# A sparse mixture of experts: routing and row scatter inside the layer norm, fixed regions of rows, a down product that gives rows, and paired value products in attention

## The chip, the cores and the metric

The kernel runs on one core of a Trainium2 chip. The metric is the device time of one launch in microseconds (us), as the median of several runs. Engines are named as the profile names them: PE is TensorE (matmul), PEld its weight loads, DVE is VectorE, ACT is ScalarE, POOL is GpSimd, SP is SyncE, which issues most DMAs.

## The reference

The reference is a small hybrid network on 32 sequences of 256 tokens with 128 channels (8192 tokens), in float32. Its layers, each added to the residual x: a two-way state-space layer, a dense feed-forward with 8 small experts, a recurrence, the feed-forward again, a local attention mixed with a latent one, a sparse mixture of experts, a causal attention, and the sparse mixture again. The change touches the two sparse mixtures and the two attentions. The mixture, cut to what matters:

```python
xn = (xf - mu) * rsqrt(var + 1e-5) * ln_gamma + ln_beta        # 8192 x 128
logits = xn @ router_w                                         # 8 experts
probs = softmax(logits); topv, topi = top_k(probs, 2); topv /= sum(topv)
for e in range(8):                                             # F = 512 hidden
    gate, up = split(xn @ gate_up_w[e])
    out += comb[:, e:e+1] * (silu(clip(gate, -10, 10)) * up @ down_w[e])
out += swiglu(xn, shared_gate_up_w, shared_down_w)             # shared, 128 hidden
```

The attention that the change touches is a softmax over 128 to 256 keys for 16 heads of width 8, per sequence and per 128 queries.

## The kernel before

The residual X and the normed U lie in SBUF for the whole program, channels on the 128 partitions and tokens along the row; 512 tokens are a tile (16 tiles). The program is a series of stages with barriers between them; inside a stage each engine runs a list written out by hand, and semaphores order the engines. Nothing reorders a list: what stands behind a waiting instruction on an engine waits too.

A sparse mixture (`l1_ffn`, twice: called ffn3 after the local attention and ffn4 after the causal one) has three stages and a fourth part:

- `layer_norm` with `route`: per tile, PE forms the mean and the variance (products with a matrix of 1/128, lines 95 and 100) and the logits (line 107), DVE subtracts the mean (129), scales (143) and shifts (146), POOL squares (175), ACT takes logarithm and exponential.
- `route_pairs` with `Choice`: after the last tile, for all 8192 tokens at once, DVE picks the two best experts, counts the tokens of each expert, and computes for each of the 16384 pairs (token, expert) a row number (`plan.slots`) in a table in DRAM, `pairs`, in which every expert's rows start at a multiple of 512. That start depends on the counts of all tokens. It also computes the expert of each of 39 blocks of 512 rows.
- `l1_experts`: chunks 0 to 15 are the shared expert on tiles of U. Meanwhile PE turns the tiles of U to rows (`turn_rows`), ACT copies them into a ring of 4 buffers `sent` (`take_rows`, line 1858), DVE adds 4 numbers for each row (`send_meta`, 1910), and POOL writes rows to `pairs` with indirect DMAs, 128 rows of 528 bytes each, 8 for a tile and 128 in all (line 1750). SP then waits for all of these DMAs and fetches the blocks (`fetch`, 1711). Per block PE turns the rows back (`turn_block`, 1811), and runs 4 chunks: gate and up products (1766 to 1768, three float32r products each), and a down product in plain float32 with the down weights loaded and 512 activations moving (1802). The result has channels on partitions: ACT copies it to `y` (`take_y`, 1876), PE turns it to rows (`turn_y`, 1820), DVE scales the rows (`scale_y`, 1946), and POOL writes them to a second table, `results`, by 4 indirect DMAs per block (1756).
- Last, the two result rows of each token are fetched, added and turned back into X.

Rows of `pairs` that no token takes must lead to spare rows of `results`: two copies of `pairs` are filled ahead of time, during the state-space layer, with zeros and a spare row number, by 6 DMAs (line 328).

In `stacked_attention` each unit of work on PE is a score product (`scores`, 2381, after a mask product 2378), the same turned over (`scores_turned`, 2407), from which ACT makes powers, and a value product (`weigh`, 2421): four heads side by side in the array, 32 columns each, with V loaded and the powers moving. A list `pending` keeps the value products two units behind. There are 384 units per attention.

Of the kernel before, what the change touches and what calls it, by code (L numbers as in the profile page):

```python
# [7 lines left out]
F32 = mybir.dt.float32  # L8
# [6 lines left out]
D = 128  # L15
# [230 lines left out]
def mamba(nc, mem, X, U):  # L246
# [14 lines left out]
    with ExitStack() as ctx:  # L261
# [63 lines left out]
        def _(sp):  # L325
            def fill(i):
                which, r = divmod(i, RING)
                sp.dma_start(mem.scratch["pairs"][which].rearrange("(i r p s) c -> r p i (s c)", r=RING, p=128, s=QUART)[r],
                             mem.empty[:, r, :, :].rearrange("p s c -> p (s c)").unsqueeze(1).to_broadcast([128, NBLK // RING, QUART * ROW])).then_inc(mem.filled, 16)

            for q in range(UNITS):
# [12 lines left out]
                if 4 <= q < 4 + 2 * RING:  # L344
                    fill(q - 4)
# [1090 lines left out]
HELD = 3  # L1436
OUT_ROWS = TOK // D
# [12 lines left out]
def fill_pairs(nc, mem):  # L1450

    empty = mem.empty
    with ExitStack() as inner:
        (zeroed, marked) = inner.enter_context(signals(nc, "fill_rows", "zeroed", "marked"))
        block = inner.enter_context(nc.Block())

        @block.vector
        def _(dve):
            nc.vector.memset(empty[:, :, :, :], 0.0).then_inc(zeroed, 1)
            dve.wait_ge(zeroed, 1 + LEAD)  # L1460
            nc.vector.tensor_copy(empty[:, :, :, ROW - 1], mem.const["spare"].rearrange("p (r s) -> p r s", r=RING)).then_inc(marked, 1)


def pairs_filled(nc, mem):

    with nc.Block() as block:
        @block.sync
        def _(sp):
            sp.wait_ge(mem.filled, 16 * 2 * RING + LEAD)
# [71 lines left out]
def route_pairs(nc, stage, mem, logits, plan):  # L1541

    with ExitStack() as ctx:
        def sb(name, *shape):
            return ctx.enter_context(nc.sbuf_tensor(stage + "_" + name, [128, *shape], F32))
        choice = Choice(nc, ctx, stage, mem, logits)
        chosen, restart, place, picked = sb("chosen", NE, NB), sb("restart", NE, NB), sb("place", NE, NB), sb("picked", NB, NE)
        running = sb("running", NE, NB)  # L1550
        past = sb("past", NE, TOK // BLK)
        needed, ends, base, ones = sb("needed", NE), sb("ends", NE), sb("base", NE), sb("ones", NE)
        slots = sb("slots", 2, NB)
        passed, count, rest = sb("passed", NBLK, NE), sb("count", NBLK), sb("rest39", NBLK)
        (made, counted, prefixed, step) = ctx.enter_context(signals(nc, stage + "_plan", "made", "counted", "prefixed", "step"))
        block = ctx.enter_context(nc.Block())
        by_expert = lambda ap: ap.rearrange("p j e -> p e j")
        by_token = lambda ap: ap.rearrange("p e j -> p j e")
        flat = lambda ap: ap.rearrange("p e j -> p (e j)")

        @block.gpsimd
        def _(pool):
            nc.gpsimd.memset(restart[:, :, :], 1.0).then_inc(made, 1)
            nc.gpsimd.memset(ones[:, :], 1.0).then_inc(made, 1)
            pool.wait_ge(made, 2 + LEAD)
            pool.sem_inc(PASSED[0], 1)
            nc.gpsimd.memset(restart[:, :, 0:1], 0.0).then_inc(made, 1)
            nc.gpsimd.tensor_copy(plan.meta[:, :, 3], mem.w["rows"]).then_inc(made, 1)

        @block.tensor  # L1570
        def _(pe):
            pe.wait_ge(counted, 1 + LEAD)
            nc.tensor.matmul(mem.bank[0][:, 0:NE], mem.w["before"], running[:, :, NB - 1], start=True, stop=True)
            nc.tensor.matmul(mem.bank[0][:, NE:2 * NE], mem.avg, running[:, :, NB - 1], start=True, stop=True).then_inc(prefixed, 1)

        @block.scalar
        def _(act):
            choice.scalar(act)

        @block.vector  # L1580
        def _(dve):
            choice.vector(dve)
            before, share = mem.bank[0][:, 0:NE], mem.bank[0][:, NE:2 * NE]
            nc.vector.tensor_tensor(by_token(chosen[:, :, :]), choice.first[:, :, :], choice.second[:, :, :], ALU.add).then_inc(step, 1)
            dve.wait_ge(made, 4 + LEAD)
            dve.wait_ge(step, 1 + LEAD)
# [1671 lines left out]
```

## Time and profile before

| | us |
|---|---|
| median of 3 runs (5911.37 to 5921.76) | 5917.6 |
| the profiled execution, its own time | 5923.9 |
| its span in the profile | 5922.0 |
| PE busy (share of the span) | 4916.7 (83%) |
| DVE busy | 4141.1 (70%) |
| ACT busy | 3098.6 (52%) |
| POOL busy | 3293.7 (56%) |

The busy shares are means over stages with different limits, so the stretches of the two mixtures and the two attentions are read by themselves. Time outside the span is 1.9 us.

### The profile page before, as it was taken

The numbers are of one execution on the slowest core, as the hardware profiler recorded it, in microseconds if no ns is written. First come the engines' busy times: TensorE is split into PE (matmuls) and PEld (weight loads), VectorE is DVE, ScalarE is ACT, GpSimd is POOL, SyncE is SP. The second block draws the span as 40 slices with busy tenths as digits, with TensorE's granted clock in tenths as the row PEclk, the third lists the DMA queues.
The fourth block names the chain that finished last, engine by engine and source line by source line (L and its number), as shares of the span: only waits on it lengthen the run. The fifth ranks groups of instructions, "written<-read, shape, count | busy, mean of one in ns | idle before, by whom it ended". The sixth has DMA issues, their size and how long they took to land. (4 is left out here: it accounts for less than half of the span.)

```text
span 5922.0 us, 78494 instructions
## 1 busy us (share of the span) xinstructions
PE 4916.7 (83%) x22329; PEld 2499.5 (42%) x22446; DVE 4141.1 (70%) x6054; ACT 3098.6 (52%) x5311; POOL 3293.7 (56%) x2373
## 2 busy tenths in 40 slices
PE   5888888888887788988797999845996899963997
PEld 1333333333333443444353555423663444432664
DVE  5999999999997573058566788633775666642775
ACT  5666666666664464245555777511332577821332
POOL 3888988898895363026343444345334565536333
PEclk8999999999999899999898999967997999976998
DMA  2234322222221002000004333012552444211555
GB/s 81 90 138 151 117 87 90 86 87 90 83 90 47 0 0 87 0 0 0 6 8 96 84 92 90 21 56 83 188 187 96 108 96 102 66 42 51 179 189 172
DMA packets 203031, 494.20 MB, mean 83 GB/s; under 512 B 32432, under 2 KB 57520, under 8 KB 191280
## 3 DMA queue, kind: packets, MB, share of 16 engines
q1 hardware_dynamic: 183536, 451.33, 24.5%
q0 software_dynamic: 18176, 37.79, 1.9%
q8 instruction: 166, 2.72, 0.2%
q14 instruction: 193, 1.58, 0.1%
q10 hardware_dynamic: 960, 0.79, 0.1%
HBM read 381.65 MB, written 108.12 MB: 83 GB/s over the span
## 5 line engine op out<-in xcount | busy, mean ns | idle before, releaser
L396 POOL TENSOR_TENSOR mamba_bu<-mamba_du,mamba_b_all 128x1024 f32<-128x1024 f32 x512 | 1198.6, 2358 | 185.3 <-PE psum L490 170.0
L667 DVE TENSOR_TENSOR_SCAN mamba_bu<-psum,mamba_bu 128x512 f32<-128x512 f32 x1024 | 1190.2, 1207 | 68.3 <-POOL mamba_bu L396 34.0
L490 PE MATMUL psum<-mamba_bu,consts 128*128 128x512 f32 x2048 | 965.4, 594 | 8.3 <-issue 5.1
L599 ACT ACTIVATE psum<-mamba_delta,A 128x510 f32<-128x510 f32 x1024 | 682.9, 683 | 388.8 <-DVE mamba_bu L667 375.7
L1756 POOL DMA_INDIRECT results<-ffn_moe_y_rows,ffn_moe_row_of x312 | 302.0, 968 | 507.2 <-DVE ffn_moe_y_rows L1946 426.3
L1871 ACT ACTIVATE ffn_moe_act<-ffn_moe_act 128x512 f32<-128x512 f32 x344 | 216.9, 631 | 688.8 <-DVE ffn_moe_act L1915 466.2
L673 DVE TENSOR_TENSOR mamba_bu<-mamba_bu,psum 128x1024 f32<-128x1024 f32 x448 | 537.3, 1199 | 5.6 <-remote 1.9
L490 PEld LDWEIGHTS psum<-mamba_bu,consts 128*128 128x128 f32 x2048 | 392.7, 192 | 347.0 <-issue 328.5
L2311 POOL TENSOR_TENSOR loc_q_bd<-loc_q_max,weights_l1a 128x512 fp32r<-128x512 f32 x256 | 274.8, 1102 | 383.4 <-DVE loc_q_max L2566 374.8
L2311 POOL TENSOR_TENSOR cau_q_bd<-cau_q_max,weights_l1b 128x512 fp32r<-128x512 f32 x256 | 258.3, 1042 | 241.4 <-DVE cau_q_max L2566 181.8
L2557 DVE TENSOR_REDUCE cau_top<-psum 128x2 f32<-128x512 f32 (+1 forms) x384 | 263.1, 692 | 181.0 <-PE psum L2381 167.4
L1915 DVE TENSOR_SCALAR ffn_moe_act<-psum 128x512 f32<-128x512 f32 x344 | 237.0, 689 | 206.5 <-PE psum L1768 129.2
L1766 PE MATMUL psum<-ffn_moe_x,ffn_moe_w_gu 128*128 128x512 f32 x624 | 372.1, 596 | 2.9 <-DVE ffn_moe_x L1905 2.9
L1750 POOL DMA_INDIRECT pairs<-ffn_moe_sent,ffn_slots x256 | 252.7, 987 | 158.4 <-ACT ffn_moe_sent L1858 82.2
L2557 DVE TENSOR_REDUCE loc_top<-psum 128x2 f32<-128x512 f32 (+1 forms) x384 | 261.1, 687 | 113.9 <-PE psum L2381 106.0
L1802 PE MATMUL psum<-ffn_moe_act,ffn_moe_w_down 128*128 128x512 f32 x624 | 318.2, 592 | 0.0
L475 PE MATMUL psum<-mamba_parts,consts 128*128 128x512 bf16 x384 | 148.4, 387 | 204.0 <-DVE mamba_bu L673 204.0
L2474 ACT ACTIVATE psum<-consts 128x512 f32<-128x512 bf16 x508 | 305.7, 602 | 16.1
L2378 PE MATMUL psum<-consts 128*128 128x256 bf16 (+1 forms) x1024 | 272.0, 306 | 41.8 <-DVE loc_top L2557 16.8
L2471 ACT ACTIVATE loc_powers<-psum 128x512 f32<-128x512 f32 x384 | 226.6, 591 | 115.2 <-PE psum L2407 114.5
L1920 DVE TENSOR_TENSOR ffn_moe_act<-ffn_moe_act,psum 128x512 f32<-128x512 f32 x344 | 235.6, 685 | 53.4 <-DMA gate_up_parts<-split_parts 30.4
L2471 ACT ACTIVATE cau_powers<-psum 128x512 f32<-128x512 f32 x384 | 225.3, 592 | 80.0 <-PE psum L2407 77.5
(426 smaller groups left out, 11023.6 us busy)
## 6 DMA issues: line engine op xcount, KB each, us to landing
mamba_b_all<-b_rows SPq DMA_DIRECT2D x256, 512.0 KB
ffn_moe_w_gu<-gate_up_parts SPq DMA_DIRECT2D x78, 1024.0 KB
pairs<-empty_rows SPq DMA_DIRECT2D x6, 3432.0 KB, 13.2
ffn_moe_got<-pairs SPq DMA_DIRECT2D x78, 264.0 KB, 3.2
ffn_moe_w_down<-in_l_moe SPq DMA_DIRECT2D x78, 256.0 KB
mamba_c_rows<-b_rows SPq DMA_DIRECT2D x32, 512.0 KB
qk_rows<-loc_qk SPq DMA_DIRECT2D x16, 1024.0 KB, 8.9
ffn_moe_back<-results SPq DMA_DIRECT2D x32, 512.0 KB, 4.8
```

Source lines behind the costliest of these rows:

```text
L396: nc.gpsimd.tensor_tensor(bu[:, J % BU, :, :], du[:, q % 2, :, :], b, ALU.mult).then_inc(bu_ready, 1)
L490: last = nc.tensor.matmul(ysum[:, h, :], mem.ident, bu[:, J % BU, h, :], start=False, stop=(n == NST - 1), skip_group_check=True)
L599: nc.scalar.activation(by_seq(dA[i % DECAYS])[:, :, 1:S], by_seq(delta[:, q % 2, h, :])[:, :, 1:S], ACT.Exp, scale=mem.A[:, q % 2, h * NST ...
L667: nc.vector.tensor_tensor_scan(bu[:, J % BU, h, :], dA[i % DECAYS], bu[:, J % BU, h, :], 0.0, ALU.mult, ALU.add).then_inc(scanned, 1)
L673: nc.vector.tensor_tensor(bu[:, J % BU, :, :], bu[:, J % BU, :, :], c_bc.unsqueeze(1).to_broadcast([D, 2, T]), ALU.mult).then_inc(weighed_ ...
L1756: nc.gpsimd.indirect_dma_start(results, bass.IndirectOffsetOnAxis(row_of[:, b % RING, s:s + 1], 0), y_rows[:, b % RING, s, :], None).then_ ...
L1766: nc.tensor.matmul(to, weights[0], x[:, i % 2, 0, :], start=True, stop=False)
L1802: nc.tensor.matmul(mem.bank[4 + i % 2], w_down[:, i % HELD, c * D:(c + 1) * D], act[:, g % 4, :], start=(c == 0), stop=(c == CH - 1)).then ...
L2311: last = nc.gpsimd.tensor_tensor(q_bd[:, s % 2, g, :, :], q_max[:, s % 2, g, :].unsqueeze(1).to_broadcast([128, GH, 128]), w["quarter"].un ...
L2471: nc.scalar.activation(powers[:, number % PT, :], mem.bank[T_BANK[number % 2]], ACT.Exp, scale=SCALE).then_inc(powers_ready, 1)
L2474: nc.scalar.activation(mem.bank[T_BANK[number % 2]].rearrange("p (h q) -> p h q", h=GH), t_seeds[number + 2].unsqueeze(1).to_broadcast([12 ...
L2557: nc.vector.tensor_reduce(top[:, s % 2, MAX_ROW + g + 32 * i:MAX_ROW + g + 32 * (i + n - 1) + 1:32], mem.bank[S_BANK[number % 2]].rearrang ...
```

## The change

Four things change.

1. `layer_norm` and `route_pairs` become one stage, `l1_front`. The logits of two tiles (a group, 8 x 128 tokens) are routed while later tiles are normed. Every expert has a fixed region of 8192 rows in `pairs` (65536 rows), so a row number needs only the counts of the tokens before it (`seen`), not the totals. ACT squares in place of POOL. The tiles are turned to rows here and stay in a whole table `sent`; the scatters of tiles 0 to 6 (`FRONT`) are issued here, the other 9 tiles' at the start of `l1_experts`. A block's place in `pairs` is now read by SP from a table (`plan.block`).
2. The fill is only zeros: one table, 34.6 MB in 16 DMAs, where it was 20.6 MB in 6. Rows at or past an expert's count are led to spare rows by `plan.limit` in `mark` (two more small DVE operations per block).
3. The down product loads 128 activations at a time as weights and moves the down weights: four products of 128 columns, rows on partitions, straight into the layout that `scale_y` reads. `take_y` and `turn_y` go.
4. In attention, value products go in pairs every second unit, and `powers` has 6 buffers for 4.

```diff
+        @block.gpsimd                                   # l1_front
+            for t in range(FRONT):
+                pool.wait_ge(rows_taken, t + 1 + LEAD)
+                pool.wait_ge(slots_ready, t // GT + 1 + LEAD)
+                pool.wait_ge(meta_ready, t // GT + 1 + LEAD)
+                plan.scatter(t)
...
+        @block.tensor
+            for t in range(NT + 3):
+                if t + 2 < NT:
+                    mean(t + 2)
+                if t < NT:
+                    var(t)
+                if 1 <= t <= NT:
+                    turn_rows(t - 1)
+                if weighted_at(t) is not None:
+                    prefix(weighted_at(t))
+                if 1 <= t <= NT:
+                    logits(t - 1)
...
+        @block.vector
+            for t in range(NT + 3):
+                if t + 2 < NT:
+                    center(t + 2)
+                if picked_at(t) is not None:
+                    choose_first(picked_at(t))
+                if weighted_at(t) is not None:
+                    put(weighted_at(t))
+                if t < NT:
+                    scale(t)
+                if picked_at(t) is not None:
+                    choose_second(picked_at(t))
+                if weighted_at(t) is not None:
+                    weight(weighted_at(t))
+            plan_blocks()
```

`picked_at` is a group's turn in steps 3, 5, 7 ..., `weighted_at` in steps 4, 6, 8 ... In `l1_experts` and below:

```diff
-            for t in range(NT):
-                pool.wait_ge(rows_sent_ready, t + 1 + LEAD)
-                pool.wait_ge(meta_ready, t + 1 + LEAD)
-                for s in range(QUART):
-                    for k in range(2):
-                        nc.gpsimd.indirect_dma_start(pairs, ...)
+            for t in range(FRONT, NT):
+                plan.scatter(t)
...
-                        pe.wait_ge(y_ready, i - 1 + LEAD)
-                nc.tensor.matmul(mem.bank[4 + i % 2], w_down[:, i % HELD, c * D:(c + 1) * D], act[:, g % 4, :],
-                                 start=(c == 0), stop=(c == CH - 1)).then_inc(down_done, 1)
+                        pe.wait_ge(y_rows_ready, i - 1 + LEAD)
+                for s in range(QUART):
+                    last = nc.tensor.matmul(mem.bank[4 + i % 2][:, s * D:(s + 1) * D], act[:, g % 4, s * 128:(s + 1) * 128], w_down[:, i % HELD, c * D:(c + 1) * D],
+                                            start=(c == 0), stop=(c == CH - 1), skip_group_check=True)
...
+                i = sp.value_load(plan.block[0:1, b:b + 1], min_val=0, max_val=NE * CHUNKS_OF - 1)
...
-        PT = 4
+        PT = 6
...
-                        while len(pending) > (2 if s < STEPS_A + T_LAG else 0):
-                            weigh(*pending.pop(0))
+                        if len(pending) > 3 or s >= STEPS_A + T_LAG:
+                            for _ in range(2 if s < STEPS_A + T_LAG else len(pending)):
+                                weigh(*pending.pop(0))
```

The POOL list of ffn3, before, from the end of the norm on: `x128` is the number of like instructions in a row, the first name is what is written.

```order
L45 ISA
L1561 UNCONDITIONAL_BRANCH
L1563 MEMSET ffn_pairs_restart 128x512
L1564 MEMSET ffn_pairs_ones 128x8
L1567 MEMSET ffn_pairs_restart 128x8
L1568 COPY ffn_meta<-weights_l_norm 128x64
L1545 UNCONDITIONAL_BRANCH
L45 ISA x2
L1741 UNCONDITIONAL_BRANCH
L1750 DMA pairs<-ffn_moe_sent,ffn_slots 19968x132 x128
L1756 DMA results<-ffn_moe_y_rows,ffn_moe_row_of 17920x128 x156
```

The same place after the change, from the start of `l1_front` on:

```order
L1594 MEMSET ffn_front_restart 128x64
L1595 MEMSET ffn_front_ones 128x8
L1596 MEMSET ffn_front_seen 128x8
L1599 MEMSET ffn_front_restart 128x8
L1600 COPY ffn_sent<-weights_l_norm 128x64
L2155 DMA pairs<-ffn_sent,ffn_slots 65536x132 x56
L1555 UNCONDITIONAL_BRANCH
L45 ISA
L1943 UNCONDITIONAL_BRANCH
L2155 DMA pairs<-ffn_sent,ffn_slots 65536x132 x72
L1951 DMA results<-ffn_moe_y_rows,ffn_moe_row_of 17920x128 x156
```

All 128 scatters stood behind the norm, the routing and their barriers; 56 now stand inside the front stage, and 72 behind its barrier.

The PE list of ffn3 around the last chunk of a block, before (the end of an up product, the turn of the block before's result, a down product, the next gate product):

```order
L1768 MATMUL psum<-ffn_moe_x,ffn_moe_w_gu 128x512
L1820 MATMUL psum<-consts,ffn_moe_y 128x128 x4
L1802 MATMUL psum<-ffn_moe_act,ffn_moe_w_down 128x512
L1766 MATMUL psum<-ffn_moe_x,ffn_moe_w_gu 128x512
L1767 MATMUL psum<-ffn_moe_x,ffn_moe_w_gu 128x512
```

The same place after:

```order
L1963 MATMUL psum<-ffn_moe_x,ffn_moe_w_gu 128x512
L1992 MATMUL psum<-ffn_moe_w_down,ffn_moe_act 128x128 x4
L1961 MATMUL psum<-ffn_moe_x,ffn_moe_w_gu 128x512
L1962 MATMUL psum<-ffn_moe_x,ffn_moe_w_gu 128x512
L1963 MATMUL psum<-ffn_moe_x,ffn_moe_w_gu 128x512
```

The four turns of `y` are gone, and each down product, once per chunk, has become four products with weights of their own.

The PE list of the causal attention, before, over one unit and the next value product:

```order
L2421 MATMUL psum<-cau_powers,cau_v 32x128 x4
L2378 MATMUL psum<-consts 128x2x128
L2381 MATMUL psum<-cau_k_bd,cau_q_st 128x512
L2407 MATMUL psum<-cau_q_bd,cau_k_st 128x512
L2421 MATMUL psum<-cau_powers,cau_v 32x128 x4
```

After, over two units:

```order
L2537 MATMUL psum<-consts 128x2x128
L2540 MATMUL psum<-cau_k_bd,cau_q_st 128x512
L2566 MATMUL psum<-cau_q_bd,cau_k_st 128x512
L2537 MATMUL psum<-consts 128x2x128
L2540 MATMUL psum<-cau_k_bd,cau_q_st 128x512
L2566 MATMUL psum<-cau_q_bd,cau_k_st 128x512
L2580 MATMUL psum<-cau_powers,cau_v 32x128 x8
```

Two value products now stand together behind every second unit.

## Rows read from the trace of the kernel before

**Rows 1.** Windows of both mixtures: engines' busy us, clock (1.00 is 2.4 GHz), DMA share.
```profile
3904.00:4090.00 186.00, 67.02 (x183) 41.29 (x183) 40.04 (x75) 28.56 (x49) 125.99 (x128) 0.64 0.20 68
...
5205.00:5257.00 52.00, 46.64 (x192) 27.78 (x192) 31.89 (x64) 21.82 (x33) 16.61 (x16) 0.93 0.00 1
...
5283.00:5466.00 183.00, 70.85 (x183) 43.35 (x183) 39.92 (x75) 28.71 (x49) 126.69 (x128) 0.64 0.20 69
5466.00:5876.00 410.00, 389.77 (x1569) 268.39 (x1569) 290.80 (x629) 136.66 (x234) 151.87 (x157) 0.97 0.50 170
```

**Rows 2.** Timeline of ffn4: first norm product, routing's end, first and last scatter.
```profile
5205.90 4.43 PE L95 MATMUL psum<-X,consts 128*128 128x512 f32 x6 [3.19 <-PEq L43]
...
5278.25 0.18 DVE L1623 TENSOR_SCALAR ffn_mark<-ffn_pairs_count 128x39 f32<-128x39 f32 x1
...
5286.00 1.04 POOL L1750 DMA_INDIRECT pairs<-ffn_moe_sent,ffn_slots  x1 [25.64 <-ACT ffn_moe_sent L1858]
...
5464.56 0.97 POOL L1750 DMA_INDIRECT pairs<-ffn_moe_sent,ffn_slots  x1 [0.30 <-issue]
```

**Rows 3.** Lines 1750 and 1756: scatter durations (ns), and idle time before 1750.
```profile
L1750 POOL DMA_INDIRECT pairs<-ffn_moe_sent,ffn_slots x256: 963/969/1458, 3907.5 to 5464.6; - x128
...
  ACT ffn_moe_sent L1858: 82.2, 6
  issue: 76.2, 250
...
L1756 POOL DMA_INDIRECT results<-ffn_moe_y_rows,ffn_moe_row_of x312: 963/969/977, 4119.6 to 5868.4; - x156
```

**Rows 4.** Groups by line in 5204:5284: busy us, mean ns, idle before.
```profile
L143 DVE SCALAR_TENSOR_TENSOR U<-U,weights_l_norm,psum 128x512 f32<-128x512 f32 x16 | 11.9, 746 | 11.4 <-ACT psum L195 11.4
...
L146 DVE TENSOR_SCALAR U<-U,weights_l_norm 128x512 f32<-128x512 f32 x16 | 8.6, 539 | 0.6
...
L727 DVE TENSOR_TENSOR ffn_pairs_hits<-ffn_pairs_hits,consts 128x512 f32<-128x512 f32 x2 | 1.4, 691 | 0.1
...
L741 DVE TENSOR_TENSOR ffn_pairs_power<-ffn_pairs_max 128x64 f32<-128x64 f32 x1 | 0.2, 226 | 0.0
```

**Rows 5.** Timeline of ffn4's blocks: turn, down product, copy of y.
```profile
5605.01 0.60 PE L1811 MATMUL psum<-consts,ffn_moe_got 128*128 128x128 f32 x4
...
5605.44 1.02 PE L1802 MATMUL psum<-ffn_moe_act,ffn_moe_w_down 128*128 128x512 f32 x2
...
5608.94 0.59 ACT L1876 ACTIVATE ffn_moe_y<-psum 128x512 f32<-128x512 f32 x1
```

**Rows 6.** The chain that ended last: start, us, what; one down product.
```profile
5546.55 0.86 PE psum L1802 x2
```

**Rows 7.** Timeline of local attention: the weight loads of V's product, the next product.
```profile
3216.59 0.97 PEld L2347 LDWEIGHTS psum<-weights_l1a,U 128*128 128x128 f32 x8 [0.20 <-issue]
...
3217.59 0.38 PE L2378 MATMUL psum<-consts 128*128 128x256 bf16 x2
```

**Rows 8.** Timeline of causal attention: value products, a mask product; the stage's last weight loads.
```profile
4904.15 0.42 PE L2421 MATMUL psum<-cau_powers,cau_v 128*32 128x128 f32 x8
4904.50 0.28 PE L2378 MATMUL psum<-consts 128*128 128x256 bf16 x1
...
4905.19 0.43 PE L2421 MATMUL psum<-cau_powers,cau_v 128*32 128x128 f32 x8
...
5177.23 0.41 PEld L2421 LDWEIGHTS psum<-cau_powers,cau_v 128*32 128x32 f32 x16 [0.24 <-issue]
```

**Rows 9.** Windows of causal attention's steady part and of local attention's.
```profile
3180.00:3780.00 600.00, 564.26 (x5042) 303.28 (x5042) 483.11 (x966) 461.57 (x997) 259.33 (x241) 1.00 0.35 83
4640.00:5150.00 510.00, 494.73 (x4415) 252.70 (x4415) 343.41 (x634) 396.87 (x726) 297.83 (x284) 1.00 0.39 96
```

**Rows 10.** Windows of the state-space layer, with fills (first) and without.
```profile
420.00:530.00 110.00, 97.06 (x231) 39.83 (x235) 106.63 (x95) 71.66 (x104) 98.13 (x45) 1.00 0.43 153
860.00:970.00 110.00, 97.07 (x231) 39.86 (x234) 106.65 (x96) 71.24 (x103) 97.94 (x45) 1.00 0.25 88
```

More of the change, by code:

```diff
@@ L1538, with l1_front @@
     pass
[L1541 removed]
+GT = 2
+GB = GT * SUB
+NG = NT // GT
+FRONT = 7
+SCATTERS = 4
+CHUNKS_OF = TOK // BLK
+def l1_front(nc, stage, mem, src, dst, affine, plan):
+    w = mem.w
+    PICKED, PLACED = 11, 20
     with ExitStack() as ctx:
@@ L1555, in route_pairs @@
-        (made, counted, prefixed, step) = ctx.enter_context(signals(nc, stage + "_plan", "made", "counted", "prefixed", "step"))
+        sq, logv = sb("sq", 2, T), sb("logv", 2, T)
+        hits, rest = sb("hits", GB, NE), sb("rest", GB, NE)
+        first, second = sb("first", GB, NE), sb("second", GB, NE)
+        max1, max2, at2 = sb("max1", GB), sb("max2", GB), sb("at2", GB)
+        power, total = sb("power", GB), sb("total", GB)
+        chosen, restart, place, running = sb("chosen", NE, GB), sb("restart", NE, GB), sb("place", NE, GB), sb("running", NE, GB)
@@ new lines, in l1_front @@
+        slots, seen, base = sb("slots", 2, GB), sb("seen", NE), sb("base", NE)
+        past = sb("past", NE, CHUNKS_OF)
+        counts, needed, ends, starts, ones = sb("counts", NE), sb("needed", NE), sb("ends", NE), sb("starts", NE), sb("ones", NE)
+        open_, begun = sb("open", NBLK, NE), sb("begun", NBLK, NE)
+        expert, begin, held, chunk = sb("of_block", NBLK), sb("begin", NBLK), sb("held", NBLK), sb("chunk", NBLK)
+        ps_mean, ps_var, rstd, small = [mem.bank[0], mem.bank[1]], [mem.bank[2], mem.bank[3]], mem.bank[4], [mem.bank[5], mem.bank[7]]
@@ new lines, in prefix @@
+            def prefix(g):
+                pe.wait_ge(counted, g + 1 + LEAD)
+                pe.wait_ge(made, 5 + LEAD)
+                to = prefixes(g)
+                nc.tensor.matmul(to, w["before"], running[:, :, GB - 1], start=True, stop=False)
+                nc.tensor.matmul(to, w["all"], seen[:, :], start=False, stop=True).then_inc(prefixed, 1)
+            mean(0)
+            mean(1)
+            for t in range(NT + 3):
[9 more added lines that the diff above has]
+                    logits(t - 1)
@@ L1576, in _, with square @@
+            pe.wait_ge(step, PLACED * NG + LEAD)
+            pe.wait_ge(small_read, NG + LEAD)
+            nc.tensor.matmul(small[0][:, 0:NE], w["all"], seen[:, :], start=True, stop=True).then_inc(summed, 1)
         @block.scalar
         def _(act):
-            choice.scalar(act)
+            def square(t):
+                act.wait_ge(centered, t + 1 + LEAD)
+                act.wait_ge(var_ready, t - 1 + LEAD)
+                nc.scalar.activation(sq[:, t % 2, :], dst[:, cols(t)], ACT.Square).then_inc(squared, 1)
@@ L1580, in _ @@
         @block.vector
         def _(dve):
[L1582 to L1586, printed above, removed]
-            nc.vector.tensor_tensor_scan(flat(running[:, :, :]), flat(restart[:, :, :]), flat(chosen[:, :, :]), 0.0, ALU.mult, ALU.add).then_inc(counted, 1)
```

358 lines of the change are left out of this document (219 added, 139 removed).

## The prediction

> **What bounds the kernel now.** I read the windows of each stage first, then the timeline at the seams, then the lines. Four stretches matter, and each has a limit of its own.
>
> In a mixture the scatter is the limit. In ffn4 the first norm product starts at 5205.90, the routing ends at 5278.43, the first scatter starts at 5286.00 and the last ends at 5465.53 [rows 2]: 259.6 us in all, of which 179.5 are scatter. In that window PE is busy 71 of 183 us, at a mean clock of 0.64 [rows 1], so PE waits. POOL's 128 scatters cost 0.969 us each plus 0.305 of idle time before each (76.2 over 250), 163 us; the rest of the 179.5 is POOL waiting for rows from ACT, 82.2 us over both mixtures, of which about 51 are the gaps ahead of the two first scatters [rows 2, 3]. ffn3's window is 186 us against 183 [rows 1], so I take both mixtures as alike.
>
> Then come the blocks: PE is busy 389.77 of 410 us at a clock of 0.97 [rows 1]. Here PE is the limit, and whatever PE does more or less counts in full.
>
> In attention PE is busy 494.7 of 510 us (causal) and 564.3 of 600 (local), ACT 397 and 462, DVE 343 and 483 [rows 9]. PE leads, but others are near.
>
> The state-space layer with a fill keeps DVE busy 106.63 of 110 us, and without one 106.65 [rows 10].
>
> **The front, term by term.** A wide DVE operation costs 0.691 us for the mean's subtraction (the price of a like operation, line 727), 0.746 for the scale and 0.539 for the shift [rows 4]: 1.98 us a tile. A group of two tiles adds 26 small operations of 64 elements or fewer (5 and 5 for the picks, 13 around them for counts and places, 3 for weights) at 0.226 us [rows 4] plus some 0.03 between dependent ones (the idle time of line 727, 0.1 us over its two, bounds it at 0.05), about 6.8. So a group costs DVE 10.8 us, and eight cost 86. With some 7 us until the first tile's root is there (an estimate from two products of 0.86 [rows 6], two wide DVE steps and three ACT steps, doubled products at the slow clock) and 10 for the drain and the block plan (20 small operations), the front ends about 103 us after its first product, where norm plus routing now take 72.5.
>
> The first group's slots are there in step 4: 7 + 5 tiles of 1.98 + 6.8, about 24 us. From there POOL has 56 x 1.274 = 71 us of scatters, and a group's 16 scatters (20.4 us) last longer than the 10.8 that DVE needs for a group, so POOL does not starve and is done at 95. From the routing's end to the first scatter it takes 7.6 us now [rows 2]; I take 6, since no row has to be turned first. The other 72 scatters start at 109 and end at 109 + 92 = 201, against 259.6. That is **-58 us per mixture, -116 in all**. What hides the front's extra 30 us of DVE time is POOL's own 71 us; POOL's gap from 95 to 109 is what is late next. The shared expert no longer waits for the ring of 4; it must fit beside the 92 us of remaining scatters. PE's 71 busy us in the scatter window [rows 1] are that work, turns included and mostly at the slow clock: it fits, with 20 to spare.
>
> Bounds. If POOL had no gap, the end would be 24 + 163 = 187: -72 each. If PE fell to 1.2 GHz throughout the front, its work per group (four wide products of 0.86 [rows 6], two turns of 0.43 [rows 5], 16 router loads of 0.111 [rows 7] and the prefix, 6.5 us at full clock) would be 13 us and pass DVE's 10.8: 18 us later, -40 each. The norm alone held 0.93 with PE busy 46.6 of 52; the scatter window fell to 0.64 with 71 of 183 [rows 1]; the front has about 6.5 of 10.8, between the two, so I take the DVE price.
>
> **The down product.** It costs 0.86 us as one product of 512 columns [rows 6]. The nearest row to the new form is V's product in attention: activations as weights, four times 128 columns of plain float32, and from its first weight load to the next product it takes 3217.59 - 3216.59 = 1.00 us; its eight loads come every 0.111 (0.97 less the last 0.19, over 7) [rows 7]. So a chunk costs 0.14 more, a block 0.56. Less goes the turn of `y`, 5605.44 - 5605.01 = 0.43 [rows 5]. **+0.13 us a block, +10 over 78 blocks.** Lower bound: the moving columns are the same 512, so 0.86 a chunk, -0.43 a block, -34. Upper bound: a load that waits for the product before it, eight times 0.111 + 0.107, 1.75 us a chunk, +243. I take the row that has the same form. ACT's copy (0.59 [rows 5]) was beside other work, except at each mixture's last block, where copy and turn stood between the last product and the last scatters: -1 each, **-2**.
>
> The Trainium skill, "TensorE: Matmul & The Clock Gate", part 3, "What overlaps and what doesn't", says that a weight load overlaps a running product only when it goes to another row group. By that rule the sum would be the upper bound. The 1.00 us of [rows 7] speaks against it.
>
> **The block fetch.** SP reads a table entry ahead of each fetch. Three blocks ahead this is hidden by 10 us of block; only the first fetch, behind the last scatter, pays: I take 1 us each (no row shows it; at 0 nothing, at most 2), **+2**. The 2 small DVE operations in `mark` lie where DVE is busy 291 of 410 us [rows 1]: nothing.
>
> **The fill** is 34.6 MB for 20.6. With fills the layer moved 153 GB/s at a DMA share of 0.43, and DVE kept its pace [rows 10]; each new fill is smaller (2.16 MB for 3.43) and 16 units have room for them: 0. Without that cover 14 MB more would be some 90 us at the 153 GB/s of that window.
>
> **Attention.** A value product takes 4904.50 - 4904.15 = 0.35 us until the next product starts, and a whole unit 4905.19 - 4904.15 = 1.04. Where two come in a row, at the stage's end, 16 weight loads take 0.41 where 8 take 0.16, so the second starts 0.25 behind the first [rows 8]. A pair saves 0.10, and 192 pairs 19 us per attention if PE alone sets the pace. PE is at 97% and 94% [rows 9], but ACT and DVE are at 78 to 81% and get their work less evenly: I take two thirds, **-13 each, -26**. Bounds: -36 each if the entry into the 32-column form, paid once less, saves as much again; +10 each if the uneven pace makes ACT late.
>
> **The sum**: -116 + 10 - 2 + 2 - 26 = -132. From the profiled 5923.9 that is 5792; the median of the three runs lies 6.3 lower, so **5786 us**.
>
> **The rivals.**
>
> *Loads not hidden (slower).* In the blocks each of the eight loads waits for the product before it: +243 in place of +10 gives 5786 + 233 = 6019. It decides against the change from a chunk price of 1.42 us on, where the blocks cost the 142 us that the rest gains. For it: the front of the row in [rows 7] is another stage, and its load is not seen ahead of its product. Against it: 1.00 us. 6%.
>
> *POOL's scatters slowed by DVE.* The front issues 56 scatters beside a DVE that is nearly always busy, where 40 of 186 us were busy before [rows 1]. Line 1750's slowest took 1.458 us; line 1756, beside a DVE busy 71%, never over 0.977 [rows 3]. At 1.46 + 0.30 for each of the 56, POOL would end at 123 and not 95, 14 us past its slack: +28 in all, 5814. The Trainium skill, "SBUF — State Buffer", "Who interferes with whom", says that POOL is blocked from writing descriptors while DVE runs a copy-like operation in its two-port mode; the front's shifts are of that kind, and line 1756's neighbours are not, so the rows do not refute it. With it I put the slow clock on PE (18 per mixture, 5822) and their sum (5850). Together 20%.
>
> *Attention loses.* If the pairs make ACT late and cost 10 each: 5786 + 46 = 5832. 8%.
>
> *The scatter is not what the blocks wait for.* If the shared expert takes over 6 us a tile, the blocks start when it ends, and the front's gain shrinks by 15 us for each us more a tile and mixture: at 8 us, +56, 5842. For it: in the scatter window it took 11 us a tile, but with POOL as what it waited for. 6%.
>
> **How the numbers follow.** The forecast with its own bounds (front -50 to -68 each, attention -6 to -22 each, down 0 to +14): 60%, 5745 to 5820. The rivals above, but the first, fill the range up to 5850 and hold 34%; the first holds 6%. The range that leaves out at most 2 in 10 is 5735 to 5842. About 0.2% (12 us) is what a measurement of this kernel tells from no change. Faster by more than that: all but the first rival and a sum of the others, 92%; the same 2%; slower 6%.
>
> **What would show it.** The first scatter about 24 us behind the first norm product, the last at about 200; scatters 1.27 us apart in the front; POOL idle 10 to 15 us once, between the 56th and the 57th; the blocks at PE's pace, a down product at 1.00 us and a block 0.13 longer; causal attention shorter by 10 to 20 us; the state-space layer unchanged. The prediction is wrong if a chunk's down product takes over 1.1 us, if the front takes over 125, or if an attention is not shorter.

## The result, and the profile after

The changed kernel takes 5883.1 us (median of 5 runs, 5875.0 to 5889.2) against 5921.8 before: 0.9936 of it, interval 0.9923 to 0.9949. It is faster by 38.6 us, not by 132. The profiled execution spans 5881.3 us for 5922.0.

The first table says where the first mixture's time lies, in us from its first norm product, as rows of the timelines give it (the second mixture agrees within 3 us). The shared expert starts with ACT's first copy for it; the first block starts with the turn of its rows; "blocks take" runs from there to the first turn of fetched result rows. "Predicted" is the prediction's own sum, with the 5 us that before takes from its last scatter to the first block.

| kernel | first scatter | shared expert starts | last scatter starts | first block | blocks take |
|---|---|---|---|---|---|
| before | 80 | 78 | 259 | 264.6 | 408.1 |
| predicted | 24 | 109 | 200 | 206 | 413 |
| after | 24.3 | 146.3 | 237.7 | 271.8 | 393.2 |

The first scatter is where it was predicted. Everything behind it is late, and the first block starts 34 us behind the last scatter, where it was 5. Windows of the profile after, around the first mixture (the stretch and its length; busy us and instructions of PE, PEld, DVE, ACT and POOL; the clock, the DMA share and GB/s; the third and fourth stretch lie inside the second):

```profile
3797.00:3821.00 24.00, 21.53 (x81) 11.82 (x82) 16.13 (x46) 13.73 (x23) 0.47 (x5) 0.87 0.00 1
3821.00:3944.00 123.00, 55.69 (x211) 38.56 (x209) 58.73 (x232) 26.98 (x52) 54.49 (x57) 0.62 0.09 31
3846.00:3862.00 16.00, 0.00 (x0) 0.00 (x0) 0.00 (x0) 0.00 (x0) 12.14 (x13) 0.59 0.15 51
3900.00:3940.00 40.00, 23.98 (x86) 18.14 (x86) 28.17 (x119) 10.57 (x21) 0.97 (x1) 0.54 0.01 4
3944.00:4035.00 91.00, 29.27 (x63) 16.76 (x63) 19.05 (x29) 11.39 (x18) 69.36 (x72) 0.59 0.27 96
4035.00:4069.00 34.00, 19.27 (x59) 11.40 (x59) 19.39 (x30) 8.15 (x14) 0.64 (x1) 0.83 0.10 28
4069.00:4456.00 387.00, 376.22 (x2349) 332.07 (x2347) 299.74 (x708) 117.44 (x195) 151.02 (x156) 0.99 0.55 175
```

From 3846 to 3862 POOL issues 13 scatters, and PE, DVE and ACT start not one instruction. From 3944 to 4035, beside 72 scatters, DVE starts 29 instructions in 91 us; behind them, 30 in 34 us. DMA is busy a quarter of the time, so its load alone is an unlikely reason; an experiment below has it at twice that share and no late tile. POOL itself is not slowed; the groups of its two scatters after, to hold against [rows 3] (mean of one in ns behind the busy time, then idle time before):

```profile
L1951 POOL DMA_INDIRECT results<-ffn_moe_y_rows,ffn_moe_row_of x312 | 302.1, 968 | 538.3 <-DVE ffn_moe_y_rows L2100 457.3 <-issue 81.0
L2155 POOL DMA_INDIRECT pairs<-ffn_sent,ffn_slots x256 | 249.5, 975 | 226.2 <-POOLq L43 85.2 <-issue 76.2 <-DVE ffn_sent L1771 64.7
```

Who is late first shows in the timeline of the shared expert beside the scatters, POOL's rows and weight loads left out (start, duration, engine, and in brackets the idle time before with what is thought to have ended it):

```profile
3996.44 0.69 DVE L2071 TENSOR_TENSOR ffn_moe_act<-ffn_moe_act,psum 128x512 f32<-128x512 f32 x1 [7.78 <-DMA gate_up_parts<-split_parts]
3997.04 0.68 DVE L2061 TENSOR_TENSOR ffn_moe_x<-U,ffn_moe_x 128x512 fp32r<-128x512 f32 x1
...
3997.78 0.79 PE L1961 MATMUL psum<-ffn_moe_x,shared_parts 128*128 128x512 f32 x1 [17.09 <-DVE ffn_moe_x L2061]
...
3998.80 0.63 PE L1963 MATMUL psum<-ffn_moe_x,shared_parts 128*128 128x512 f32 x1
...
4000.08 0.63 PE L1963 MATMUL psum<-ffn_moe_x,shared_parts 128*128 128x512 f32 x1
4000.51 1.91 PE L1983 MATMUL psum<-ffn_moe_act,shared_down 128*128 128x512 f32 x2
4010.40 0.69 DVE L2066 TENSOR_SCALAR ffn_moe_act<-psum 128x512 f32<-128x512 f32 x1 [12.07 <-DMA split_whole<-in_l_moe]
4011.12 0.63 ACT L2038 ACTIVATE ffn_moe_act<-ffn_moe_act 128x512 f32<-128x512 f32 x1 [14.13 <-DVE ffn_moe_act L2066]
4018.80 0.63 ACT L2031 ACTIVATE ffn_moe_x<-U 128x512 fp32r<-128x512 f32 x1 [7.04 <-DMA gate_up_parts<-split_parts]
4018.87 0.69 DVE L2071 TENSOR_TENSOR ffn_moe_act<-ffn_moe_act,psum 128x512 f32<-128x512 f32 x1 [7.78 <-DMA gate_up_parts<-split_parts]
```

PE starts 0.06 us behind DVE's L2061, and ACT 0.03 behind DVE's L2066: waits on DVE end at once. The clip L2066 waits for the three gate products, which started at 3997.78 to 3998.80, and starts at 4010.40. The multiply L2071 waits for the up product of 4000.08 and starts at 4018.87. The DMAs named in the brackets landed long before; the trace's record of the semaphore that the last gate product raises stands at 4010.37. So each wait that ends late is a wait for TensorE, whose rows give a start and a modelled end. Such a tile takes 22.4 us (4018.87 less 3996.44); behind the scatters a tile takes 3.7. In the front it is the same. DVE's subtraction L1702 at 3863.12 is the 11th of the stage and waits for the 11th mean product, which stands 31 us ahead of it, at 3832.18; the 12th stands at 3842.52:

```profile
3832.18 1.10 PE L1616 MATMUL psum<-X,consts 128*128 128x512 f32 x2
...
3842.52 2.05 PE L1616 MATMUL psum<-X,consts 128*128 128x512 f32 x2
...
3860.83 0.97 POOL L2155 DMA_INDIRECT pairs<-ffn_sent,ffn_slots  x1 [0.30 <-issue]
3863.12 0.69 DVE L1702 TENSOR_TENSOR U<-X,psum 128x512 f32<-128x512 f32 x1 [25.17 <-issue]
```

The records of the semaphores say what is late. Eight router products of 8 columns, which start from 3831.10 on, count as done at 3858.19, 19.7 us behind the turn ahead of them (3838.46), 2.5 us for each; the subtraction that waits for the next mean product, two instructions of 512 columns, starts 4.9 us later. The next twenty PE instructions (a turn, a prefix, eight router products, the 12th mean and a variance) start from 3839.22 to 3845.22, and their five semaphores stand between 3866.63 and 3866.87, 5 us behind the end of the scatters at 3861.80. The sixteen instructions behind the turn do not run in these 0.24 us: the four of the mean and the variance start 0.85 us or more apart. So TensorE must have done them before, and what comes late beside the scatters is their completion, by which I mean the moment from which the semaphore lets others go on.

The blocks went the other way. A chunk's first gate product, its down product and the next gate product, where [rows 6] showed 0.86 for the two records of before:

```profile
5575.92 0.48 PE L1961 MATMUL psum<-ffn_moe_x,ffn_moe_w_gu 128*128 128x512 f32 x1
...
5577.40 1.05 PE L1992 MATMUL psum<-ffn_moe_w_down,ffn_moe_act 128*128 128x128 f32 x8
5578.20 0.47 PE L1961 MATMUL psum<-ffn_moe_x,ffn_moe_w_gu 128*128 128x512 f32 x1
```

From gate product to gate product a chunk takes 2.28 us; before it was 2.24 (5605.90 to 5608.14). From turn to turn of `got`, over the 30 blocks from the 6th on, a block takes 9.57 us for 9.86.

### The profile page after: what moved, and what is told of

The parts are those of the page before. It is cut to its first block and busy times, and to the rows that moved or that the text cites. A ratio compares the mean times of both kernels' runs of the same rounds, so it can differ in the third digit from the quotient of the medians.

```text
span 5881.3 us, 82272 instructions
## 1 busy us (share of the span) xinstructions
PE 4835.3 (82%) x23949; PEld 2665.8 (45%) x24066; DVE 4199.7 (71%) x6527; ACT 3084.9 (52%) x5279; POOL 3255.9 (55%) x2343
## 5 line engine op out<-in xcount | busy, mean ns | idle before, releaser
L2066 DVE TENSOR_SCALAR ffn_moe_act<-psum 128x512 f32<-128x512 f32 x344 | 236.6, 688 | 198.8 <-PE psum L1963 97.3
L2155 POOL DMA_INDIRECT pairs<-ffn_sent,ffn_slots x256 | 249.5, 975 | 226.2 <-POOLq L43 85.2
L1992 PEld LDWEIGHTS psum<-ffn_moe_w_down,ffn_moe_act 128*128 128x128 f32 x2496 | 320.3, 191 | 19.3
L1992 PE MATMUL psum<-ffn_moe_w_down,ffn_moe_act 128*128 128x128 f32 x2496 | 328.0, 274 | 0.0
L2071 DVE TENSOR_TENSOR ffn_moe_act<-ffn_moe_act,psum 128x512 f32<-128x512 f32 x344 | 235.2, 684 | 101.8 <-DMA gate_up_parts<-split_parts 53.2
L1961 PE MATMUL psum<-ffn_moe_x,ffn_moe_w_gu 128*128 128x512 f32 x624 | 273.9, 439 | 4.3 <-DVE ffn_moe_x L2061 3.7
```

The lines of the kernel that those rows point to most:

```text
L1961: nc.tensor.matmul(to, weights[0], x[:, i % 2, 0, :], start=True, stop=False)
L1992: last = nc.tensor.matmul(mem.bank[4 + i % 2][:, s * D:(s + 1) * D], act[:, g % 4, s * 128:(s + 1) * 128], w_down[:, i % HELD, c * D:(c + ...
```

## The experiments

**The three edits apart.** Kernels made from the one before: only the new down product; only the paired values; both, with the old front. The pairs and the down product are the change's own lines:

```diff
-        PT = 4
+        PT = 6
...
-                nc.tensor.matmul(mem.bank[4 + i % 2], w_down[:, i % HELD, c * D:(c + 1) * D], act[:, g % 4, :],
-                                 start=(c == 0), stop=(c == CH - 1)).then_inc(down_done, 1)
+                for s in range(QUART):
+                    last = nc.tensor.matmul(mem.bank[4 + i % 2][:, s * D:(s + 1) * D], act[:, g % 4, s * 128:(s + 1) * 128],
+                                            w_down[:, i % HELD, c * D:(c + 1) * D], start=(c == 0), stop=(c == CH - 1), skip_group_check=True)
+                last.then_inc(down_done, 1)
```

> The kernel before with nothing but the sparse experts' down product in its new form. Theory (its 128-column weight loads are hidden behind the products): a block is shorter by the turn of y, some 0.37 us, 78 blocks and the two last turns give 29 us: 5893. Rival (the term as I predicted it, a chunk at 1.00 us): 5932.

Measured: 5894.4 us against 5916.7, 0.9953 (0.994 to 0.9966). The blocks take 397.3 and 396.3 us for 408.1 and 406.8. The theory holds: 22 us off.

> The kernel before with nothing but the paired value products and six buffers of powers. Theory (the pairs alone made the two attentions what they are after the change): the local one 24 to 25 us shorter, the causal one 1 us longer, 23 us in all: 5899. Rival (the local attention gained from something else of the change): both attentions within 5 us of before: 5917 to 5922.

Measured: 5899.8 us, 0.9971 (0.996 to 0.9982): 17 us off. From the first to the last value product the local attention takes 606.7 us for 622.9 and the causal one 546.8 for 549.9; in the kernel with the down product alone these are 622.8 and 550.8. So the pairs are worth 16 and 3 us. The theory's split was off, for it counted the stretch ahead of the local attention's first value product, which came 16 us earlier in the profile of the down product too, where nothing before it is edited. Single profiles differ by that much there; terms are compared inside their stretches from here on.

> The kernel before with the new down product and the paired value products, but with its own front (norm, then routing, then all scatters). Theory (the fused front brings nothing, and the two other edits add up): 29 and 23 us off, 5870, faster than the changed kernel by some 13 us. Rival (the fused front brings a part of the gain): not faster than the changed kernel's 5883.

Measured: 5876.2 us, 0.9926 (0.9913 to 0.9939): 40.5 us off, as the two apart (22 and 17). It is as fast as the changed kernel, which carries the fused front on top: the front brought nothing.

**What sets the pace of the completions: semaphore updates, or instructions?** Eight PE instructions and three updates make a shared tile, and its 22.4 us could be the price of the one or of the other. Two kernels add six instructions to a tile and no update, first wide ones, then ones of 8 columns:

```diff
+                for _ in range(2 if g < NT else 0):
+                    product(mem.bank[g % 2], gate_weights(g), i)
                 product(mem.bank[g % 2], gate_weights(g), i).then_inc(gate_ready, 1)
```

> The changed kernel with each shared tile's gate product made three times, six more products of 512 columns a tile and not one more semaphore update. Theory (beside the scatters TensorE's products run at their pace, and only its semaphore updates come late, one per 7 to 8 us): a shared tile beside the scatters takes 22 to 25 us as before, and a tile behind them some 2.6 us more. Rival (beside the scatters each product itself takes some 2.8 us): a shared tile beside the scatters takes 39 us.

```diff
+                for _ in range(6 if g < NT else 0):
+                    nc.tensor.matmul(mem.bank[g % 2][:, 0:8], gate_weights(g)[0], x[:, i % 2, 0, 0:8], start=True, stop=True)
                 product(mem.bank[g % 2], gate_weights(g), i).then_inc(gate_ready, 1)
```

> The changed kernel with six more products of 8 columns in each shared tile, without a semaphore update. The six products of 512 columns lengthened a tile beside the scatters from 22.4 to 37 us. Theory (what TensorE takes beside the scatters is a price per instruction, some 2.5 us whatever its size): a tile beside the scatters takes 37 us again. Rival (a price per column, that is a slow read of data): 22.4 to 23 us.

Timeline of the wide ones, DVE's clip (L2068) and multiply (L2073) behind the products:

```profile
3976.77 0.69 DVE L2073 TENSOR_TENSOR ffn_moe_act<-ffn_moe_act,psum 128x512 f32<-128x512 f32 x1 [5.01 <-DMA gate_up_parts<-split_parts]
...
3978.12 0.79 PE L1961 MATMUL psum<-ffn_moe_x,shared_parts 128*128 128x512 f32 x1 [8.45 <-issue]
...
4004.70 0.69 DVE L2068 TENSOR_SCALAR ffn_moe_act<-psum 128x512 f32<-128x512 f32 x1 [26.64 <-DMA split_whole<-in_l_moe]
...
4013.19 0.69 DVE L2073 TENSOR_TENSOR ffn_moe_act<-ffn_moe_act,psum 128x512 f32<-128x512 f32 x1 [7.80 <-DMA gate_up_parts<-split_parts]
```

and of the small ones:

```profile
3985.01 0.69 DVE L2073 TENSOR_TENSOR ffn_moe_act<-ffn_moe_act,psum 128x512 f32<-128x512 f32 x1 [4.98 <-issue]
...
3986.36 1.44 PE L1973 MATMUL psum<-ffn_moe_x,shared_parts 128*128 128x8 f32 x6 [12.41 <-DVE ffn_moe_x L2063]
...
4022.81 0.69 DVE L2073 TENSOR_TENSOR ffn_moe_act<-ffn_moe_act,psum 128x512 f32<-128x512 f32 x1 [7.78 <-DMA gate_up_parts<-split_parts]
```

A tile takes 36.4 and 37.8 us: (36.4 - 22.4) / 6 = 2.3 and 15.4 / 6 = 2.6 us for each instruction, whether of 512 or of 8 columns. My theory of a price per update fell with the first run, and a price per moving column, that is a slow read of data, with the second. Each added product brings a load of 128 weight columns, so the load and the product are not told apart. The whole took 5944.6 and 5921.1 us, one run each.

**Which transfers do it?** The scatter without its index list, 128 rows to 128 rows side by side; the rows of the results at fixed places, so that the output is not the reference's:

```diff
-                    nc.gpsimd.indirect_dma_start(mem.scratch["pairs"], bass.IndirectOffsetOnAxis(plan.slots[:, k, j:j + 1], 0),
-                                                 plan.sent[:, j, :], None).then_inc(plan.scattered[t % SCATTERS], 16)
+                    n = 2 * j + k
+                    nc.gpsimd.dma_start(mem.scratch["pairs"][n * 128:(n + 1) * 128, :], plan.sent[:, j, :]).then_inc(plan.scattered[t % SCATTERS], 16)
```

> The changed kernel with each of the 256 scatters as a plain GpSimd transfer of the same 128 rows to 128 rows that lie side by side, and with the rows of the sparse experts' results put to fixed places, so that what is added back is not the reference's. Theory (the index form, in which the 128 addresses are looked up, holds TensorE up): a shared tile beside them takes 4 us, and the first block starts 60 us or more earlier in each mixture. Rival (any dense train of GpSimd transfers of this size does it): tiles beside them still take over 10 us.

Measured: 5638.5 us, one run. Windows of its front behind the first scatter and of its shared expert, and the transfers' group:

```profile
3812.00:3885.00 73.00, 48.24 (x209) 33.27 (x207) 58.01 (x231) 26.41 (x50) 30.13 (x56) 0.73 0.16 53
3885.00:3942.00 57.00, 38.27 (x119) 22.54 (x120) 38.52 (x58) 19.59 (x33) 38.24 (x72) 0.95 0.53 169
```

```profile
L2156 POOL DMA_DIRECT2D pairs<-ffn_sent x256 | 137.0, 544 | 136.5 <-POOLq L43 80.2 <-DVE ffn_sent L1771 55.3 <-issue 1.0
```

The same bytes leave POOL faster, 72 transfers in 38 us, and a shared tile beside them takes 3.7 us. So neither the bytes nor POOL's being at work holds TensorE up, but something that the form with an index list brings: the list, the scattered places that it writes to, or the 0.97 us on POOL for 0.54. These were not tried apart.

**Does a pause help?** After four, eight or sixteen scatters POOL waits until they have landed (the edit for eight):

```diff
                     nc.gpsimd.indirect_dma_start(mem.scratch["pairs"], bass.IndirectOffsetOnAxis(plan.slots[:, k, j:j + 1], 0),
                                                  plan.sent[:, j, :], None).then_inc(plan.scattered[t % SCATTERS], 16)
+                if j % 4 == 3:
+                    nc.gpsimd.wait_ge(plan.scattered[t % SCATTERS], 16 * 2 * (t // SCATTERS * QUART + j % QUART + 1))
+                    nc.gpsimd.sem_inc(PASSED[0], 1)
```

> The changed kernel with POOL waiting after every four scatters until they have landed. Theory (TensorE falls behind some ten scatters into an unbroken train, and a pause lets it catch up): shared tiles beside the scatters take some 4 us, the front some 105 us; a train takes 5.1 us and a pause about 2, so POOL is the limit again and ends at about the same time as now, 4035 to 4060 in the first mixture; the blocks start 5 to 35 us earlier, the whole is 5815 to 5875. Rival (scatters and TensorE share something by turns, pauses or not): tiles stay above 15 us, and the pauses come on top, slower than 5883.

> The same with trains of eight. Theory: as eight are fewer than the ten or so after which TensorE falls behind, tiles stay at some 4 to 6 us, 16 pauses cost 32 us a mixture, and the blocks start 30 to 40 us earlier: 5800 to 5825. Rival: 5883 or more.

> The changed kernel with a wait for landing after every sixteen scatters. Theory (TensorE falls behind some ten scatters into a train and takes 2.5 us an instruction from there): in each train of 20.4 us some 8 are lost to a tile, so tiles alternate, 3.7 and 12; eight pauses less than with eights take 17 us off POOL's end: 5790 to 5850. Rival (no threshold, the loss grows with the train's length from its start): tiles of 10 us throughout.

And a pause that waits for nothing, a fill of a scratch tile in place of the wait:

```diff
-                    nc.gpsimd.wait_ge(plan.scattered[t % SCATTERS], 16 * 2 * (t // SCATTERS * QUART + j % QUART + 1))
+                    nc.gpsimd.memset(still[:, :], 0.0).then_inc(rested, 1)
+                    nc.gpsimd.wait_ge(rested, t + 1)
```

> The changed kernel with trains of eight and, in place of the wait for landing, a fill of a scratch tile of 1024 columns on POOL, some 1 us. Theory (TensorE needs time without scatters, not their landing; in the changed kernel it caught up within 1 to 2 us of a train's end): tiles beside the scatters take 4 to 6 us, and pauses that are 1 us shorter than those of the wait take 14 us off each mixture: 5780 to 5790. Rival (what counts is that the transfers have landed): tiles above 10 us, 5840 to 5885.

| kernel | us | ratio to before, interval | first scatter | shared expert starts | last scatter starts | first block | blocks take |
|---|---|---|---|---|---|---|---|
| trains of 4, landed | 5875.0 | 0.9927 (0.9913 to 0.994) | 25.3 | 132.8 | 260.3 | 266.2 | 394.1 |
| trains of 8, landed | 5810.8 | 0.9822 (0.9808 to 0.9835) | 25.3 | 119.8 | 229.2 | 234.9 | 393.9 |
| trains of 16, landed | 5844.9 | 0.9876 (0.9861 to 0.9891) | 25.3 | 142.7 | 244.8 | 250.5 | 395.1 |
| trains of 8, fill | 5798.2 | 0.9792 (0.9778 to 0.9805) | 24.4 | 116.4 | 220.3 | 226.1 | 395.1 |
| plain transfers | 5638.5 | one run | 24.9 | 98.3 | 136.4 | 155.2 | 394.2 |

With trains of four and eight nearly every shared tile beside the scatters takes 3.7 us, and POOL sets the end again. Timeline of the kernel with the fill: POOL, and DVE's clip of three tiles in a row, 3.66 and 3.70 us apart:

```profile
3940.84 0.69 DVE L2066 TENSOR_SCALAR ffn_moe_act<-psum 128x512 f32<-128x512 f32 x1 [0.46 <-issue]
...
3942.39 0.97 POOL L2157 DMA_INDIRECT pairs<-ffn_sent,ffn_slots  x1 [0.31 <-issue]
...
3943.35 0.97 POOL L2160 MEMSET ffn_still<- 128x1024 f32 x1
...
3944.50 0.69 DVE L2066 TENSOR_SCALAR ffn_moe_act<-psum 128x512 f32<-128x512 f32 x1 [0.46 <-issue]
3945.14 0.97 POOL L2157 DMA_INDIRECT pairs<-ffn_sent,ffn_slots  x1 [0.82 <-issue]
...
3948.20 0.69 DVE L2066 TENSOR_SCALAR ffn_moe_act<-psum 128x512 f32<-128x512 f32 x1 [0.46 <-PE psum L1963]
```

From the end of one scatter to the start of the next this pause takes 1.78 us (2.07 in the front) in place of 0.30, and that is enough: the landing does not matter. The fill was to save 28 us over the wait and saved 12.6 (17 by the two ratios, for each was taken beside its own runs of before), since it makes the pause only some 0.35 us shorter. Nor did TensorE catch up within 1 to 2 us of a train's end, as I had expected: in the changed kernel it took 5 us and more. So a pause seems to keep the delay from building up, rather than to let TensorE catch up; that was not tested. With sixteen the front is as long as without pauses (142.7 and 146.3), more than the 8 us a train that I expected, while shared tiles lose little (3.1 to 7.7 us from multiply to multiply): from which scatter between the eighth and the sixteenth on TensorE falls behind was not settled, and the two stages differ in it.

**Two more.** Eight tiles of scatters in the front and no pause in the last three:

> The changed kernel with trains of eight scatters and a wait for their landing, but no pause in the last three tiles, and eight tiles of scatters in the front in place of seven. Theory (with pauses POOL sets the end: 12.3 us for eight scatters and a pause of 2.1; the shared tiles are done when the last three tiles of scatters start): one tile of scatters less behind the front's end, 10 us a mixture, and two pauses of 2.1 us: 28 us off the 5811 of the trains of eight, 5783. Rival (the unbroken train at the end holds the last shared tiles up, or the front ends later by what moves into it): 5800 to 5830.

Measured: 5808.6 us, 0.9813 (0.98 to 0.9827), 2 us below the trains of eight, which is within the noise, and not 28. The rival holds: POOL's last scatter in the front, and not DVE, ends the front, and what moved into it made it longer (132.2 for 119.8). Timeline of POOL at that seam, with 11.66 us for the change of stage:

```profile
3921.38 0.97 POOL L2155 DMA_INDIRECT pairs<-ffn_sent,ffn_slots  x1 [0.30 <-issue]
...
3934.01 0.96 POOL L2155 DMA_INDIRECT pairs<-ffn_sent,ffn_slots  x1 [11.66 <-POOLq L43]
```

And the pauses under the old front:

```diff
                                                      sent[:, t % SENT, s, :], None).then_inc(scattered[t % SENT], 16)
+                pool.wait_ge(scattered[t % SENT], 16 * 2 * QUART * (t // SENT + 1))
+                pool.sem_inc(PASSED[0], 1)
```

> The kernel before with the new down product and the paired value products (5876), and a wait for landing after each tile's eight scatters. Theory (there POOL is the limit already, and TensorE's late tiles cost only the two gaps of some 9 us in POOL's train): 16 pauses of 2.1 us less those gaps, 16 us a mixture more, 5908; so the fused front is worth 97 us once TensorE keeps its pace. Rival (the pauses are worth as much without the fused front): 5804.

Measured: 5910.3 us, 0.9983 (0.9974 to 0.9993), 34 us slower than without them. There POOL is the limit, and the pauses only lengthen its train. With the same pauses the fused front is worth 5910.3 - 5810.8 = 99.5 us, 95 by the two ratios.

The kernel with trains of eight and the fill beats both: 5798.2 us, 85 less than the changed one.

## Why the prediction was wrong, step by step

**The front: the step that failed.** Predicted -116. Measured: 40.5 us off without the fused front and 38.6 with it, so nothing that the runs can tell; inside the stretches the first block comes 7 and 8 us later than before. The working assumed that the other engines keep their pace beside the scatters: "What hides the front's extra 30 us of DVE time is POOL's own 71 us", and of the shared expert "it fits, with 20 to spare". In its place the runs show that beside an unbroken train of indexed scatters TensorE's instructions complete at some 2.5 us each, and all who wait for them wait that long. In the front that cost 146 - 109 = 37 us, past the 125 that were to prove the prediction wrong. In the shared expert it made 16 tiles take 125.5 us, so that it ended 34 us behind the last scatter and not 20 ahead. That this term was at fault is shown by the runs; why TensorE is held up is not.

The rest of the front's sum stood. The first scatter was forecast at 24 and came at 24.3; the front at 103 with its next stage at 109, and with plain transfers the next stage starts at 98.3. The last scatter was forecast at 200. With the fill it starts at 220.3; that kernel has 14 pauses ahead of it, each 1.5 to 1.8 us longer than a usual gap, and without these 22 us it would be at 198. So, by this estimate, -116 is about what the front is worth where TensorE keeps its pace; 95 to 99.5 were measured with pauses.

The sign was in the trace of before. I had noted that a shared tile took 11 us in the scatter window, and set it down to POOL, for which it waited; and I counted POOL's wait for ACT [rows 3] as a price of the old order of work. Of its 82.2 us some 51 lie ahead of the two first scatters, as I wrote; the other 31 are four stops of some 8 us, at the 48th and the 104th scatter of each mixture. In the first of them (POOL goes on at 3976.75) ACT's copy L1858 starts at 3975.26, when the semaphore of TensorE's turn stands, at 3975.24, though the turn's rows start at 3972.39; and the tiles around such stops take 27 to 31 us from multiply to multiply, where most others beside the scatters take 8 to 11. The step to ask for was what ACT itself waited for.

**The down product: right place, wrong sign.** Predicted +10, measured -22 (e_down). The term that was mis-sized is the chunk: 0.14 us more, from V's product in [rows 7]; measured 2.28 for 2.24, 0.04 more. Four of these less the turn of 0.43 are -0.27 a block, and 78 blocks -21. The lower bound, -34, was the nearer one. The upper bound, that each weight load waits for the product before it, is refuted. The Trainium skill, "TensorE: Matmul & The Clock Gate", part 3, "What overlaps and what doesn't", lets a load overlap only where it goes to another row group; by that, with the prediction's estimate of 1.75 us, a chunk would have cost 0.89 us more. The trace does not agree, with its 0.04.

**Attention: a third less in all, and another split.** Predicted -13 each, at the least -6. The pairs gave 16 us in the local attention and 3 in the causal one by the stretches, 17 in all by the medians. Why the causal one gains so little was not tried.

**Small terms.** The block fetch: from the last scatter's start to the first block's turn it takes 5.8 us with the fill, where e_down has 5.0 and 5.2; +1 was forecast, from no row. Up to the local attention the profile after is 5.7 us ahead of before, so the fill costs nothing to be seen. The tail's -2 can't be told apart in the blocks' 11 us.

**The rivals.** Weight loads not hidden: refuted. Scatters slowed by DVE: refuted, at a mean of 0.975 us and at most 1.272 beside a busy DVE. The Trainium skill, "SBUF — State Buffer", "Who interferes with whom", has POOL's descriptors wait for DVE's two-port operations; in these rows POOL's scatters keep their pace, and it is TensorE's completions that come late, while DVE is idle (3846 to 3862). A slow PE clock: it did sink, to a mean of 0.59 and 0.62, but from 3900 to 3940 it was at 0.54, nearly all of it at 1.2 GHz, and with one scatter beside it DVE was busy 28 of 40 us. Attention loses: refuted. The rival that the blocks wait for the shared expert came true: at 125.5 / 16 = 7.8 us a tile I had it at 5842, with 6%; what it lacked is that the front is held up by the same cause, 37 us a mixture.

By terms: -132, +116 for the front, -32 for the down product, +9 for attention give -39; measured -38.6. That the total is off by no more than 93 us is in part luck: the down product's miss went the other way.

**What stays open.** Why TensorE's completions alone are held up, and not those of DVE and ACT; what the indexed form shares with them; from which scatter on; and whether the recording of the trace has a part in it, for no run tells. The blocks' own scatters come in fours, and no tile beside trains of four was late.

## What to carry to other kernels

Work that is moved beside a train of indexed GpSimd transfers may not cost what it costs elsewhere: look at the pace of the other engines in a stretch where such a train runs, and follow a wait on to what the waited-for engine waits for. A matmul row that stands at its usual time does not show that its result was to be had then: compare it with the start of what waits for it. Break such trains: a pause of 1.5 us after every eighth gave 85 us here, for one instruction of fill. An edit whose gain hangs on overlap should be tried with the overlapped partner made cheap (here, plain transfers), which shows at once whether the sum or the overlap is wrong.

## What the runs showed of the hardware that was not expected

An unbroken train of indexed scatters (0.97 us each, 0.30 between) holds TensorE's completions at some 2.5 us an instruction, of 8 columns as of 512, though the instructions' rows start at their usual pace; once the train had ended, the five semaphores of twenty instructions came within 0.24 us. DVE's and ACT's instructions beside it keep their 0.69 and 0.63 us and follow each other within 0.1 us. Plain GpSimd transfers of the same bytes, 0.54 us each, do nothing of the kind. A matrix product of 128 moving columns in plain float32 hides the load of the next 128 columns of weights almost fully: eight loads and products take 0.80 us until the next product starts, and a chunk with them 0.04 more than with two wide ones.
